# Differential attention: heads' outputs transposed before their norm, squares on GpSimd, and the last sums by matmul in the last batch

## The reference, cut to what matters

```python
x = L0_attn_x                                   # [8, 1024, 512], 16 heads of 32
q1, q2 = jnp.split(q, 2, axis=-1)               # the same for k; v keeps 32
a1 = softmax(q1 @ k1.T * scale); a2 = softmax(q2 @ k2.T * scale)
a = a1 - lam * a2
out = jnp.einsum('bhst,bhtd->bhsd', a, v)
rms = jnp.sqrt(jnp.mean(out * out, axis=-1, keepdims=True) + EPS)
out_n = out / rms * norm_w[None, :, None, :] * (1.0 - LAMBDA_INIT)
out_cat = out_n.reshape(b, H * s, HD)
out_final = out_cat.transpose(0, 2, 1).reshape(b, s, e)
x = x + out_final @ wo
x = x + ffn(layernorm(x))       # ternary weights, low-rank part, squared ReLU
```

## Time and profile before

| | us |
|---|---|
| median of 3 runs | 3933.77 (3931.87 to 3934.77) |
| the profiled execution | 3933.88, span 3932.1 |
| PE busy | 3799.9 (97%) |
| DVE busy | 3184.3 (81%) |
| ACT busy | 2835.5 (72%) |
| POOL busy | 2.0 |

### The profile page before, as it was taken

One profiled execution on the slowest core, in us unless ns is written; L12 is line 12 of the kernel. 1 busy time (PEld: TensorE's weight loads), 2 busy tenths in 40 slices (PEclk: granted clock), 3 DMA queues, 4 the chain that ended last, 5 costly groups with the idle time before them and its releaser, 6 DMA issues.

```text
span 3932.1 us, 57774 instructions
## 1 busy us (share of the span) xinstructions
PE 3799.9 (97%) x22088; PEld 2106.5 (54%) x22088; DVE 3184.3 (81%) x3046; ACT 2835.5 (72%) x3597; POOL 2.0 (0%) x14
## 2 busy tenths in 40 slices
PE   6799999999999999999999999989899999999999
PEld 5344444444444444444444444333378888888887
DVE  5699999999999999999999999999855555555554
ACT  2598888888888888888888888999733333333333
POOL 0000000000000000000000000000000000000000
PEclk9899999999999999999999999999999999999999
DMA  5445444445445445444444435434101010101010
GB/s 195 129 99 117 100 113 109 102 109 109 111 100 115 106 96 122 103 113 105 103 109 108 114 88 117 100 73 94 45 10 43 22 44 22 44 22 44 22 44 22
DMA packets 225845, 338.26 MB, mean 86 GB/s; under 512 B 86704, under 2 KB 107184, under 8 KB 225008
## 3 DMA queue, kind: packets, MB, share of 16 engines
q1 hardware_dynamic: 225520, 333.88, 34.9%
HBM read 180.72 MB, written 150.99 MB: 84 GB/s over the span
## 4 chain that ended last, share of the span: by engine, by line
PE 80%; DVE 10%; ACT 6%; issue 3%; DMA 1%; SPq 1%; DVEq 0%; ACTq 0%
PE ps L568 18%; PE ps L541 13%; PE ps L672 12%; PE ps L652 12%; DVE acc L1204 8%; PE ps L480 7%; PE ps L483 5%; PE ps L628 4%; ACT pr L905 4%; PE ps L589 3%; PE ps L657 1%; PE ps L604 1%; PE ps L456 1%; PE ps L702 1%; PE ps L692 1%
## 5 line engine op out<-in xcount | busy, mean ns | idle before, releaser
L905 ACT ACTIVATE pr<-ps 128x1024 f32<-128x1024 f32 x2048 | 1988.7, 1029 | 225.5 <-PE ps L541 220.8
L1204 DVE TENSOR_TENSOR acc<-acc,pr 128x2048 f32<-128x2048 f32 x768 | 1755.2, 2285 | 48.6 <-ACT pr L905 22.1
L568 PE MATMUL ps<-pr,vst 128*32 128x512 f32 x8192 | 1020.4, 600 | 0.0
L541 PE MATMUL ps<-qst,kst 50*128 50x512 f32 x4096 | 786.6, 455 | 58.3 <-ACT pr L905 40.1
L541 PEld LDWEIGHTS ps<-qst,kst 50*128 50x128 f32 x4096 | 329.5, 184 | 716.0 <-ACT pr L905 531.5
L1057 ACT ACTIVATE rb<-ps,scf 128x512 f32<-128x512 f32 x256 | 176.3, 689 | 390.0 <-PE ps L657 390.0
L568 PEld LDWEIGHTS ps<-pr,vst 128*32 128x32 f32 x8192 | 207.7, 109 | 438.7 <-issue 424.3
L672 PE MATMUL ps<-tP,hh_ 128*128 128x512 f32 x1024 | 404.3, 395 | 1.9 <-DVE hl_ L1419 1.9
L652 PE MATMUL ps<-yh,tT 128*128 128x512 f32 x1024 | 404.9, 395 | 0.0
L652 PE MATMUL ps<-yl,tT 128*128 128x512 f32 x1024 | 399.9, 391 | 0.0
L672 PE MATMUL ps<-tP,hl_ 128*128 128x512 f32 x1024 | 399.1, 390 | 0.0
(11 more groups left out here) (154 smaller groups left out, 3491.9 us busy)
## 6 DMA issues: line engine op xcount, KB each, us to landing
qst<-q_scratch SPq DMA_DIRECT2D x128, 384.0 KB, 6.3
kst<-k_scratch SPq DMA_DIRECT2D x128, 384.0 KB, 9.2
q_scratch<-stg SPq DMA_DIRECT2D x168, 256.0 KB
k_scratch<-stg SPq DMA_DIRECT2D x168, 256.0 KB
xin<-in_L_attn_x_dram SPq DMA_DIRECT2D x16, 1024.0 KB, 5.6
v_scratch<-vsg SPq DMA_DIRECT2D x64, 256.0 KB, 3.0
vst<-v_scratch SPq DMA_DIRECT2D x128, 128.0 KB, 5.4
xr<-in_L_attn_x_dram SPq DMA_DIRECT2D x64, 256.0 KB
```

What stands on the lines that cost most here:

```text
L541: ins = e.matmul(ps[:, 2 * c + hh, :], kst[rows, r, j, t * 128:(t + 1) * 128], qst[rows, r, j, c * 512:(c + 1) * 512], start=True, stop=True)
L568: ins = e.matmul(ps[32 * c4:32 * c4 + 32, 4 + j, :], vst[:, r, t, 32 * hh:32 * hh + 32], pr[:, sl, c, hh, :], start=(t == 0), stop=(t == 7 ...
L905: e.activation(pr[:, sl, c, :, :], ps[:, 2 * c:2 * c + 2, :], ACT.Exp, scale=SCALE).then_inc(s_exp, 1)
L1204: e.tensor_tensor(acc[:, j, :], old, new, ALU.add).then_inc(s_add, 1)
```

## The change

`ot` is now transposed as it is (TensorE, d = 3, into bank 5), and ScalarE copies the result into `on` (d = 4), with positions on partitions. GpSimd squares it (`sq`), VectorE sums each group of 32 columns (d = 5), ScalarE takes Ln and Exp of 16 columns (d = 6), VectorE multiplies `on` by the result (d = 7), ScalarE makes `oth` out of `on` (d = 8, which is d = 0 of the next pair) and VectorE `otl` (d = 9, d = 1 of the next pair). `norm_w` goes into the addition of x, which becomes a scalar_tensor_tensor. The matmul with `blk`, the squares on ScalarE, the product `on` and the wide Ln and Exp are gone.

In the last batch VectorE leaves out the addition for t = 7 of each half, and the sum's matmuls take the eighth block from `pr` (four more matmuls for each sum). The low-rank loads are issued one pair later, the memsets of GpSimd stand in its loop over the pairs.

```diff
+def pe_adds(P):
+    return P >= NPAIR - NP
...
+            for X in range(NPAIR):
...
+                e.wait_ge(s_raw, X + 1)
+                if X:
+                    e.wait_ge(s_ssq, X)
+                e.tensor_tensor(sq[:], on[:], on[:], ALU.mult).then_inc(s_osq, 1)
...
                 if j == 0:
                     e.wait_ge(s_xtl, turned(P))
-                    if P >= 2:
-                        e.wait_ge(s_otl, P - 1)
                 elif P:
-                    e.wait_ge(s_rmln, P)
+                    e.wait_ge(s_raw, P)
...
-            e.wait_ge(s_add, n_add(X, j, 7))
+            e.wait_ge(s_add, n_add(X, j, 6 if pe_adds(X) else 7))
...
+            if pe_adds(X):
+                gg = 16 * X + 8 * j + 7
+                e.wait_ge(s_exp, n_half(gg, 1))
+                for hh in range(2):
+                    for c in range(2):
+                        c4 = 2 * hh + c
+                        t = e.matmul(ps[32 * c4:32 * c4 + 32, bk, :], ones[:], pr[:, gg % NPB, c, hh, :], start=False,
+                                     stop=True, skip_group_check=True)
...
-                e.wait_ge(s_osq, X + 1)
-                e.wait_ge(s_pt, 2 * X + 2)
+                e.wait_ge(s_ot, X + 1)
...
-                    t = e.matmul(ps[:, 5, c], blk[:], sq[:, c], start=(n == 0), stop=True, skip_group_check=True)
...
-                    t = e.transpose(ps[:, 4, kk * 128:(kk + 1) * 128], on[:, kk * 128:(kk + 1) * 128], ident[:])
+                    t = e.transpose(ps[:, 5, kk * 128:(kk + 1) * 128], ot[:, kk * 128:(kk + 1) * 128], ident[:])
...
-            if d == 2 and half == 0:
-                e.wait_ge(s_ot, X + 1)
+            if d == 4 and half == 0:
+                e.wait_ge(s_tr, X + 1)
+                if X:
+                    e.wait_ge(s_otl, X)
...
+                e.activation(on[:], ps[:, 5, :], ACT.Copy).then_inc(s_raw, 1)
+            if d == 6 and half == 1:
+                e.wait_ge(s_ssq, X + 1)
+                e.activation(ms[:, 1, :], ms[:, 0, :], ACT.Ln, bias=eps6, scale=1.0 / HD).then_inc(s_rmln, 1)
+                e.wait_ge(s_rmln, X + 1)
...
+                e.activation(ms[:, 2, :], ms[:, 1, :], ACT.Exp, scale=-0.5).then_inc(s_rmex, 1)
-            if d == 7 and half == 1:
-                e.wait_ge(s_tr, X + 1)
+            if d == 8 and half == 1:
+                e.wait_ge(s_on, X + 1)
...
-            if t == 0:
+            if t == 0 or (t == 7 and pe_adds(P)):
                 return
...
+            if d == 5 and half == 1:
+                e.wait_ge(s_osq, X + 1)
...
+                e.tensor_reduce(ms[:, 0, :], sq[:].rearrange("p (g d) -> p g d", d=HD), AX.X, ALU.add) \
+                    .then_inc(s_ssq, 1)
+            if d == 7 and half == 1:
                 e.wait_ge(s_rmex, X + 1)
...
+                e.tensor_tensor(heads, heads, ms[:, 2, :].unsqueeze(2).broadcast_to([128, 16, HD]), ALU.mult) \
+                    .then_inc(s_on, 1)
...
-                e.tensor_tensor(xr[:], ps[:, 7, :], xr[:], ALU.add).then_inc(s_x2v, 1)
+                e.scalar_tensor_tensor(out=xr[:], in0=ps[:, 7, :], scalar=nw[:, p:p + 1], in1=xr[:], op0=ALU.mult,
+                                       op1=ALU.add).then_inc(s_x2v, 1)
```

More of the change, by code:

```diff
@@ L38, in n_half, with probabilities_read @@
     return 2 * gg + c + 1
+def pe_adds(P):
+    return P >= NPAIR - NP
 def n_add(P, j, t):
-    return (2 * P + j) * 7 + max(t, 1)
+    return (2 * P + j) * 7 - (2 * (P - NPAIR + NP) + j if pe_adds(P) else 0) + max(t, 1)
+def probabilities_read(e, s_add, s_sum, f):
+    P, j, t = f // 16, (f // 8) % 2, f % 8
+    if t == 7 and pe_adds(P):
+        e.wait_ge(s_sum, 2 * P + j + 1)
+    else:
+        e.wait_ge(s_add, n_add(P, j, t))
 def sum_bank(P, j):
@@ L253, in gpsimd_program @@
                             channel_multiplier=-1).then_inc(s_pool, 1)
[L255 to L260, removed]
+            for X in range(NPAIR):
+                if X == NPAIR - NP:
+                    for r in range(2):
+                        e.wait_ge(s_vsg[r], 16 * 2 * NC)
+                    e.memset(fba[:], 0.0).then_inc(s_pool, 1)
+                    e.memset(vrep[:], 0.0).then_inc(s_pool, 1)
+                if X == NPAIR - 1:
+                    e.wait_ge(s_sum, 2 * NPAIR)
+                    e.memset(on1[:], 1.0).then_inc(s_pool, 1)
+                e.wait_ge(s_raw, X + 1)
+                if X:
+                    e.wait_ge(s_ssq, X)
+                e.tensor_tensor(sq[:], on[:], on[:], ALU.mult).then_inc(s_osq, 1)
         def sync_x(e, C):
@@ L427, in sync_program @@
                         sync_weights(e, 1)
-                    if d == 1 and P == NPAIR - NP:
+                    if d == 1 and P == NPAIR - NP + 1:
                         sync_low_rank(e)
@@ L589, in pe_sum @@
                     t = e.matmul(ps[32 * c4:32 * c4 + 32, bk, :], ones[:], acc[:, j, (2 * c + hh) * 512:(2 * c + hh + 1) * 512],
-                                 start=True, stop=True, skip_group_check=True)
+                                 start=True, stop=not pe_adds(X), skip_group_check=True)
+            if pe_adds(X):
[6 more added lines that the diff above has]
+                                     stop=True, skip_group_check=True)
             t.then_inc(s_sum, 1)
@@ L1296, in vector_program @@
         def vector_program(e):
-            e.memset(blk[:], 0.0).then_inc(s_cst, 1)
             e.memset(ones[:], 1.0).then_inc(s_cst, 1)
@@ L1301, in vector_program @@
                 e.memset(kst[64 * hh + 32:64 * hh + 64, :, :, :].bitcast(F32), 1.0).then_inc(s_cst, 1)
-            e.wait_ge(s_cst, 1)
-            for i in range(4):
-                e.memset(blk[32 * i:32 * i + 32, 32 * i:32 * i + 32], 1.0).then_inc(s_cst, 1)
             for n in range(5):
@@ L1403, in vector_program @@
             dve_low_rank_weights(e, 3)
-            dve_post(e, NPAIR - 1, 4, 1)
             for n in range(6, 11):
                 dve_ln_step(e, 2 * B, n)
-            for k in range(4):
-                dve_turn_rows(e, 0, k)
+            dve_turn_rows(e, 0, 0)
+            dve_turn_rows(e, 0, 1)
+            dve_post(e, NPAIR - 1, 5, 1)
+            dve_turn_rows(e, 0, 2)
+            dve_turn_rows(e, 0, 3)
             dve_post(e, NPAIR - 1, 7, 1)
             dve_low_rank(e, 0)
+            dve_post(e, NPAIR - 1, 9, 1)
             for n in range(NB2):
```

64 lines of the change are left out of this document (22 added, 42 removed).

## The result

The changed kernel takes 3940.6 us (median of 20 runs, 3937.9 to 3947.7), the kernel before 3934.3 in the same comparison (3931.9 to 3937.6): ratio 1.0018, 95% interval 1.0011 to 1.0025. The prediction was 3937, range 3916 to 3951. The total came out nearly right by luck: what the prediction charged for GpSimd's square was not paid, and costs that it did not have came to about as much. The twenty executions of the changed kernel spread over 9.8 us, those of the kernel before over 5.7; the mean granted TensorE clock is 0.993 of full speed in the shortest of the twenty and 0.990 in the longest.

What follows compares the result with a forecast made beforehand. TensorE bounds ordinary pairs, VectorE the layer-norm pair, and in the last batch ScalarE and TensorE wait for each other. 6.7 - 2.2 - 2.4 + 4.5 - 3.1 = +3.5 us on 3933.9 gave 3937 us, range 3916 to 3951.

Steps and rivals of the forecast that it cites:

- VectorE sets pair 0: In the one pair of heads in four with layer norm, VectorE sets the time; the added reduction costs +0.6 us.
- c = 0.7 in pairs 0 and 1: GpSimd's square makes one VectorE addition 0.7 us late in the pair with layer norm and in the next.
- the first rival: GpSimd's square does not hold VectorE up, or is as short as a memset: 3920.6 us in all; chance 25%.
- 24c: Part of the total, 3920.6 + 24c us, that depends on c, what one GpSimd square costs VectorE.
- The upper bound of 1.7 us: Longest time considered for GpSimd's square, twice the one-input time, against 1.3 us expected.
- Predicted +0.64: Pair behind the one with layer norm: 0.6 and 0.7 us more VectorE work give 42.4 against 41.76 us.
- Pairs 2 and 3: Last two pairs of each four, set by TensorE: -0.52 us, with 0.34 new waiting for `stg`, and -0.86 us.
- The last batch: Each sum's four more matmuls cost +0.9 us, other changes bring -1.1 a pair; +4.5 us for 7 pairs.
- The way out: Leaving attention: VectorE's last addition goes, -2.2 us; wide Exp and `on` leave the path, -0.9; together -3.1 us.
- The sum: All terms of the whole kernel together: +3.5 us on 3933.9, which gives 3937 us.
- the forecast with c = 0: Forecast for the whole kernel if GpSimd's square costs VectorE nothing: 3920.6 us.

## Why the prediction came out as it did

- **VectorE sets pair 0, and one more instruction costs 0.60 us.** Right in the kernel before: 43.75 of 43.86 us busy with one reduction more, all else as before. In the changed kernel the way over `stg`, TensorE and ScalarE is as long at d = 4, which the prediction did not have.
- **The square and c = 0.7 in pairs 0 and 1.** The step that failed. The square is 1.04 us, not 1.3, so the hold-up is 0.25 and 0.44; and taking it away wholly changed neither pair, by the squares on ScalarE and by the memset. As a price of the square c is 0, the condition of the first rival; yet its 3920.6 did not come. The term 24c charged 16.8 us for it. (The upper bound of 1.7 us, twice the time with one input, should be 1.8; nothing hangs on it.)
- **What came in its place.** In pair 1 it is the other half of the edit, `otl` ahead of `stg`. The prediction worked TensorE's slack against `stg` out for pair 2 (0.68 us) and for pair 1 only added up VectorE's work. There TensorE waits 0.41 and 0.42 us, which eats the 0.86 of `blk`; with `otl` behind the second `stg` the pair is 0.57 shorter. Predicted +0.64, measured +0.43, for another reason; that the two are near is luck.
- **Pairs 2 and 3.** -0.34 and -0.73 against -0.52 and -0.86. The new wait for `stg` in pair 2 is there, 0.24 to 0.32 us against 0.34. Beyond it TensorE comes 0.44 us earlier at d = 7, where the transposes stood, and then takes small waits: in pair 1 four score matmuls take 0.89 instead of 0.73 us, and the sum's matmuls begin 1.04 instead of 0.88 behind those of the values. Whether ScalarE is what it waits for was not tested.
- **The fall of the clock.** Not forecast: +6.1 us in the pairs 0 of the profiled execution, and some 1.5 more in pair P = 1, where waits for ScalarE stood before it. The stop of 1.66 us follows from the prediction's own numbers (0.76 of the earlier trace rows, 0.42 that TensorE is earlier, 0.60 that `stg` is later, 1.78 in all), but it was taken for an idle time that costs nothing in a pair that VectorE sets.
- **The last batch.** Right in both halves as numbers: the sums +1.70 by themselves (predicted +1.8), the rest -1.2 (-1.1). That ScalarE's square, the copy and the transposes make up the 1.2 was not tested one by one, and the rest is worth that much only beside the longer sums: with all additions on VectorE it brings 42.49 to 42.44.
- **The way out.** -2.4 against -3.1. The last addition is worth 2.3 us (predicted 2.2), between the kernel with all additions on VectorE and the changed one. The wide Exp and `on` were to bring 0.9, and the norm's part brings 0.1 (the kernel with all additions on VectorE against the kernel before). The split depends on the order: by the kernel with the sums alone the addition is worth 1.7 and the norm's part 0.7. The chain of waits there has now the product `on` of pair 62, moved from d = 4 to d = 7:

```profile
2837.33 2.11 issue
2839.44 0.68 DVE on L1248
2840.13 0.67 DVE xr L1258
```

  That this is where the missing 0.2 to 0.8 us went is read from the chain and wasn't tested.

- **The sum.** Luck. The 16.8 us for the square were not paid. In their place, against the forecast with c = 0, stand some 3 us more in the twelve pairs 0 apart from the falls (10.3 against 7.2), 5.9 in the pairs 1, 3.6 in the pairs 2 and 3, and the 6.1 of the falls: 18.7 us that the prediction did not have.

## What to carry to other kernels

An instruction added to a full engine costs its start-to-start distance; one that is put ahead of what another engine waits for costs in every stage where that engine is the bound, and the place can be worth more than the work (17 us here with equal work, 6 of them by the clock). For each edit ask up to which instruction of the busy engine the other one waits, and count the work before that one only. A stop of TensorE in a stage that another engine sets isn't free either, once it is long enough for the clock to fall.

## What the runs showed of the hardware

- A GpSimd tensor_tensor of 128x512 fp32 with inputs in SBUF takes 1.04 us. Issued during a VectorE addition with two inputs in SBUF it first waits for that one's end (1.05 us), and the next such VectorE instruction waits for it: additions took 2.53 and 2.74 instead of 2.28 us, and a product of 4 columns, behind another such instruction of GpSimd, took 1.01 instead of 0.15. A memset on GpSimd (0.52 us) did neither. Two tensor_scalars of VectorE on `xin`, with one tensor in SBUF as input, took 1.29 instead of 0.99 us beside GpSimd's `otl`.
- TensorE's granted clock fell to about one half for some 3 us behind a single stop of 1.64 to 1.71 us in a stretch in which TensorE was otherwise busy, in 21 of 60 cases; at the same place behind stops of up to 1.29 us in none of 84. In pair P = 1 it fell behind waits of 0.65 us and less.
